# Self attention on one Trainium2 core: score products moved behind the projections on TensorE, their row maxima moved behind the probability split on VectorE

## What is computed

```
q = einsum('btc,hcd->bhtd', x, Wq) + bq;  k, v likewise
scores = einsum('bhtd,bhsd->bhts', q, k) * D ** -0.5
probs  = softmax(scores + causal)          # causal: -inf above the diagonal
y      = einsum('bhts,bhsd->bhtd', probs, v)
x      = x + y @ Wo + bo
```

## Time and profile before

| | us |
|---|---|
| median of 3 runs (1720.44 to 3871.68) | 1721.91 |
| span of the profiled execution | 1720.1 |
| PE busy (TensorE matmul) | 1570.6 (91%) |
| PE weight loads | 1288.7 (75%) |
| DVE busy | 1271.6 (74%) |
| ACT busy | 837.5 (49%) |
| POOL busy | 369.6 (21%) |

### The profile page before, as it was taken

How to read it: one execution, slowest core, us unless ns; L and a number is a source line. 1 busy time by engine, 2 the same in 40 slices (tenths; PEclk the granted TensorE clock), 3 DMA queues, 4 the chain that set the end, 5 groups by cost and what they waited for, 6 DMA issues and landing times. The chain is left out here.

```text
span 1720.1 us, 30317 instructions
## 1 busy us (share of the span) xinstructions
PE 1570.6 (91%) x10720; PEld 1288.7 (75%) x10720; DVE 1271.6 (74%) x2429; ACT 837.5 (49%) x1976; POOL 369.6 (21%) x329
## 2 busy tenths in 40 slices
PE   7886989999999999999999758999999999999996
PEld 5665778778787877878787636877878787878785
DVE  4354687777878778787777857979797979797963
ACT  4443577676776767676676721323232322222220
POOL 2240111021110212111021142313132323232310
PEclk9998999999999999999999978999999999999998
DMA  9998443433434324333432341222212222122000
GB/s 317 330 295 249 89 109 75 99 93 93 116 68 126 74 66 120 89 97 74 110 79 70 111 197 62 74 74 74 73 73 73 73 73 73 73 73 79 19 19 19
DMA packets 75155, 178.52 MB, mean 104 GB/s; under 512 B 9392, under 2 KB 9520, under 8 KB 71344
## 3 DMA queue, kind: packets, MB, share of 16 engines
q1 hardware_dynamic: 75056, 177.07, 34.9%
HBM read 76.37 MB, written 50.33 MB: 74 GB/s over the span
## 5 line engine op out<-in xcount | busy, mean ns | idle before, releaser
L772 DVE TENSOR_REDUCE a_neg_max<-a_score 128x1 f32<-128x384 f32 (+3 forms) x352 | 224.2, 637 | 119.7 <-PE a_score L887 119.0
L676 ACT ACTIVATE a_probs<-a_score,a_neg_max 128x384 f32<-128x384 f32 (+3 forms) x512 | 267.1, 529 | 86.6 <-DVE a_neg_max L772 49.6
L779 DVE TENSOR_TENSOR a_pt_lo<-a_turned,a_pt_hi 128x512 f16<-128x512 f32 (+1 forms) x352 | 223.1, 634 | 12.1 <-ACT a_pt_hi L685 10.6
L896 PE MATMUL a_turned<-ident,a_probs 128*128 128x128 f32 x1280 | 210.7, 283 | 21.6 <-ACT a_probs L676 21.4
L685 ACT ACTIVATE a_pt_hi<-a_turned 128x512 f16<-128x512 f32 (+1 forms) x352 | 197.0, 560 | 64.6 <-PE a_turned L896 64.2
L622 POOL TENSOR_TENSOR a_y<-a_y_sum,a_y_rec 128x128 f32<-128x128 f32 x128 | 51.1, 399 | 661.4 <-DVE a_y_sum L793 661.4
L885 PE MATMUL a_score<-a_stack 96*128 96x384 f32 (+3 forms) x512 | 182.4, 393 | 1.3 <-DMA a_stack<-a_qk 1.3
L916 PE MATMUL a_out_y<-a_v,a_pt_hi 128*128 128x96 bf16 x1280 | 142.5, 209 | 20.8 <-DVE a_pt_lo L779 20.2
L916 PEld LDWEIGHTS a_out_y<-a_v,a_pt_hi 128*128 128x128 f16 x1280 | 98.8, 98 | 81.6 <-issue 44.1
L896 PEld LDWEIGHTS a_turned<-ident,a_probs 128*128 128x128 f32 x1280 | 134.6, 141 | 24.4 <-ACT a_probs L676 24.1
L1133 POOL TENSOR_TENSOR b_probs<-b_probs,b_row_scale 128x1024 f32<-128x1024 f32 x32 | 61.0, 1905 | 361.9 <-DVE b_row_scale L1333 361.9
(11 more groups left out here) (177 smaller groups left out, 4171.3 us busy)
## 6 DMA issues: line engine op xcount, KB each, us to landing
a_stack<-a_qk SPq DMA_DIRECT2D x384, 128.0 KB, 2.4
m_dram<-c_m_out SPq DMA_DIRECT2D x8, 2048.0 KB, 13.2
vw_dram<-shared SPq DMA_DIRECT2D x32, 512.0 KB, 8.4
shared<-m_dram SPq DMA_DIRECT2D x8, 2048.0 KB, 8.1
b_vw_raw<-vw_dram SPq DMA_DIRECT2D x8, 2048.0 KB, 8.4
c_w_raw<-w_group_dram SPq DMA_DIRECT2D x7, 1280.0 KB, 11.2
x_in<-x_dram SPq DMA_DIRECT2D x8, 1024.0 KB, 5.4
a_x_res<-x_dram SPq DMA_DIRECT2D x8, 1024.0 KB, 7.7
```

Source lines behind the costliest of these rows:

```text
L676: ins = nc.scalar.activation(probs[:, n % 2, k * width:(k + 1) * width], score[n % 2][:, k * width:(k + 1) * width], ACT.Exp, bias=neg_max ...
L772: nc.vector.tensor_reduce(neg_max[:, c:c + k], score[n % 2][:, 0:k * width].rearrange("p (h s) -> p h s", h=k), AX, ALU.max, negate=True). ...
L779: nc.vector.tensor_tensor(pt_lo[:, n % 2, 0:width], turned[n % 2][:, 0:width], pt_hi[:, n % 2, 0:width], ALU.subtract).then_inc(pt_ready, 1)
L896: last = nc.tensor.transpose(turned[n % 2][:, c * P:(c + 1) * P], probs[:, n % 2, c * P:(c + 1) * P], ident[:, :])
```

## The change

Three things, all in `self_attention`; nothing is added to or taken from the work.

1. PE: in each unit the steps of the projections are issued ahead of `scores(m + 2)` instead of behind it.
2. PE: inside `scores` all score products of a unit come first, then all causal products. Only the first product of the unit has `start`, only the last has `stop`, since the bank's flags are cleared once.
3. DVE: `row_max(m + 2)` is issued behind `outputs(m - 2)` and `probs_lo(m)` instead of ahead of them.

```diff
@@ DVE, half
                     for kind, n in completed(beside[max(0, m - 1):m]):
                         low_part(it, kind, n)
-                    if unit_at(b, n0 + m + 2):
-                        row_max(*unit_at(b, n0 + m + 2))
                     if unit_at(b, n0 + m - 2):
                         outputs(*unit_at(b, n0 + m - 2))
                     probs_lo(b, n0 + m)
+                    if unit_at(b, n0 + m + 2):
+                        row_max(*unit_at(b, n0 + m + 2))
@@ PE, scores
                 for k, j in enumerate(heads):
                     at = k * width
                     nc.tensor.matmul(score[n % 2][:, at:at + width], st[:, 0, j, i * P:(i + 1) * P], st[:, 1, j, 0:width],
-                                     start=True, stop=False)
+                                     start=k == 0, stop=False)
+                for k, j in enumerate(heads):
+                    at = k * width
                     last = nc.tensor.matmul(score[n % 2][:, at + i * P:at + width], ident_bf[:, :], causal_bf[:, :],
-                                            start=False, stop=True)
+                                            start=False, stop=k == len(heads) - 1)
@@ PE, half
                     turn(b, n0 + m)
+                    for step in beside[m]:
+                        step_of_product(it, *step)
                     if unit_at(b, n0 + m + 2):
                         scores(*unit_at(b, n0 + m + 2))
-                    for step in beside[m]:
-                        step_of_product(it, *step)
                     if unit_at(b, n0 + m - 1):
                         weigh(*unit_at(b, n0 + m - 1))
```

## The result

The changed kernel takes 1825.8 us (median of 4 runs, 1824.66 to 1827.03), against 1721.2 before: ratio 1.0616, 95% interval 1.0601 to 1.0631. Forecast were 1822 us in a range of 1806 to 1846. The ratio leaves out one run of the kernel before that took 3871.68 us; it still counts in the median of 1721.2 us.

A forecast was written before the change was run, and what follows sets the result against it. One round through ACT and DVE per unit was taken to bound the changed kernel: 1720.1 + 96.9 + 1.6 + 2 = 1820.6 us, with 1.8 us up to the median 1822, range 1806 to 1846.

The forecast's parts named there:

- The ring: Self attention: exps, probs_hi, probs_lo, row_max close once per unit on ACT and DVE; 2.55 us per unit, +96.9 us.
- everything beside: Self attention: 1.6 us for DVE's other work in a round plus 2 us for later scores and delayed transposes.
- The term for late scores and full VectorE rounds: Late scores and PE overruns 2 us, bounds 0 and 18; unit 18's crowded DVE round 1.6 us, at most 5.
- The dense stretch: A batch's 21 units with projections: hardly loses, 53 us before and about 53.4 after.
- Where the loss lies: Second half of each batch about 10 us, projection-free half at the end some 22, also first half of batch 0.
- TensorE's term: PE's order: some 28 us less work, bounds 0 and 40, from 18 and 10; counted as 0 in the time.
- the first rival: Self attention: PE stays the bound and its saving comes through, 1720 - 28 = about 1692 us; chance 2%.
- the third rival: Light units: more lost than the round; half clock adds 14 us, with late scores 1840 to 1855 us; chance 12%.
- Signs to look for: Timeline: 2.6 us rounds, exponentials waiting for maxima, PE waiting well over 100 us at transposes; against: clock under 1.00.

The follow-up runs named there:

- the maximum alone: Kernel before with only row_max moved behind outputs and probs_lo on VectorE, TensorE's order old; 1825.9 us, ratio 1.0620.
- the grouping alone: Kernel before with only the causal products of a unit grouped behind its score products on TensorE; 1715.8 us, ratio 0.9958.

## Why the prediction was right

**The ring and its price: right.** The round was summed as 28.03 us per quad. The start-to-start times of the exponentials in the changed kernel add up to 3.35 + 2.87 + 2.73 + 2.38 + 2.14 + 2.14 + 2.28 + 2.38 + 3 x 2.62 = 28.13 us for an undisturbed quad. From the first exponentials (183.1 us) to the last (1086.33) it is 903.2 us against 795.6 before: +107.6 us. The sum had +96.9, and 3.6 for everything beside.

**Some of the closeness is luck.** 107.6 is 7 us more than the 100.5 us counted; outside self attention's steps the changed execution was 4 us shorter (1.8 us ahead of the first exponentials, 2.3 behind the last). No run here gives a cause; the first exponentials start anywhere from 183.1 to 189.1 us in the traces of this case. By the start-to-start times the part beyond +96.9 is 3.2 us since the links of a quad are 0.1 us longer than read, some 3.5 us of overruns (0.5 us a batch in units 1, 20 and 23, where one unit, 18, was named), and 3.7 us in batch 0, whose unit 1 takes 5.24 us and whose units 18 and 19 together take 1.3 us too much: 10.4 us where 3.6 were counted. The term for late scores and full VectorE rounds was too small; its bounds of 5 and 18 us held it.

**The dense stretch: nearly.** From the transposes of unit 0 to those of unit 21 of one batch it took 51.55 us before (590.04 to 641.59) and 53.17 now (638.14 to 691.31): +1.6 us where +0.4 was forecast. Its 53.4 us for the changed kernel was right; its 53 us for the kernel before was the length of the window of the earlier trace rows, not of these 21 rounds.

**Where the loss lies: partly as forecast.** By the starts of the exponentials, the second halves (units 22 to 43) lose 7.6 us each, where about 10 were forecast, the half without projections 21.6 (forecast 22), and the first half of batch 0 11.3. The other seven first halves, said to hardly lose, lose 3.1 us each, 21.5 in all; about half of that is the 1.6 us above. The places' errors cancel, because the round was summed over all 351 steps and not place by place.

**TensorE's term: the sizes at the places were right, the worth was not.** The unit of the earlier trace rows now reads:

```profile
655.36 0.64 PE L901 MATMUL a_turned<-ident,a_probs 128*128 128x128 f32 x4
655.75 0.48 PE L44 MATMUL a_gemm<-a_xt_hi,w_self_hi 128*128 128x512 f32 x1
656.07 0.40 PE L44 MATMUL a_gemm<-a_xt_lo,w_self_hi 128*128 128x512 f32 x1
...
657.25 0.39 PE L888 MATMUL a_score<-a_stack 96*128 96x512 f32 x1
657.48 0.23 PE L892 MATMUL a_score<-a_causal_bf,a_ident_bf 128*128 128x128 bf16 x1
657.55 0.21 PE L921 MATMUL a_out_y<-a_v,a_pt_hi 128*128 128x96 bf16 x1
```

The first projection matmul behind the transposes takes 0.32 us and the score 0.23, where it was 0.32 and 0.31: 0.08 us saved, as written; and the score starts 0.24 us after the last projection matmul, which was a sign to look for. What costs it is the first 512-column fp32r matmul behind 128-column ones (transposes or causal products), of which the unit had two and now has one; whether width or type makes the difference these runs don't tell. In the changed kernel that is worth nothing, since no PE instruction is in the ring: the maximum alone costs as much as the full change. But the first rival's price, "1720 - 28", was wrong: without the ring the two TensorE changes give 1724.9 us. Two things in it failed. The saving was too large even where PE sets the time: both changes take 1.5 us off units 0 to 21 and 0.3 us off units 31 to 44, some 14 us over the eight batches. And not all of a batch is such a place: what was saved ran into the gap at the loop's turn, the transposes ahead of the scores and the lower clock.

**The clock: the third rival's mechanism came, without its price.** The light stretches ran at 0.86 and the last half at 0.68. It was guessed that this could add up to 14 us. The ring, which has no PE instruction in it, hid nearly all of it: in the last half, at a clock of 0.68, all units but one keep the start-to-start times that they have in the middle batches.

**Signs to look for.** Seen: the ring at 2.62 us, maxima that no longer wait for scores (4.8 us, before 119.0), exponentials that wait for the maximum (337 times). Missed: PE's wait at the transposes was forecast "well over 100 us" and is 98.4; the clock inside the stage fell, which was listed as a sign against the forecast, and wasn't one. The last half was forecast at "about 56 us instead of 34" and took 53.6 instead of 32.1 by the exponentials: both 2 us too long, the difference right.

## What to carry to other kernels

Look for rings that go through two in-order engines: follow an instruction to what waits for it and to what stands behind it in its engine's list, until the same instruction of a later unit comes up, and divide the length of the round by the number of units it advances. Swapping two neighbours (here a maximum and a split on VectorE) can take that number from two to one, and then a pair of engines at 46 and 70% busy sets the time, whatever the fullest engine does; start-to-start times from the old trace gave the length of the round to half a per cent (28.03 against 28.13 us) and its cost to a tenth (96.9 against 107.6). Time saved on the fullest engine is worth only what the places behind it don't take back: try the parts of a reordering apart.

## What was not expected of the hardware

- At the turn of the hardware loop TensorE stands still for about 2.5 us (2.50 to 2.68 from start to start in the kernel before, at five turns); ahead of unit 22 of the three other batches, where the loop isn't turned, it is 0.87. With the steps ahead of the scores and no ring it is 3.3 to 3.9 us at the turns and 0.67 else.
- The DMA records tell more of this gap. The trace has a queue "instruction" with packets of 16 KB, and at every turn one of them is under way: in the rows above from 642.61 to 643.79 us before and from 643.21 to 644.18 with both TensorE changes. TensorE's transposes start 1.54 and 1.51 us behind its end, and 1.50 to 1.73 us behind it at all 70 turns of the 14 kernels, though the exponentials that they need had ended at 643.48 and 642.93. The packets elsewhere in the stage come with no such gap (in the kernel before at most 0.95 us). So the gap is most likely TensorE waiting for its own instructions. It grew because the packet starts later: 0.14 us ahead of TensorE's last matmul before, 0.81 us behind it in the other kernel. Why it starts later is not shown.
- At the gaps of 2.4 to 2.8 us the granted clock fell to half at one of five turns before, and at two of five with the grouping alone. At each of the gaps of 2.8 to 3.9 us, in all kernels, it fell to half within 2.3 us of the transposes' start, ahead of it or behind. In the two windows shown around a turn (640 to 660 us with both TensorE changes, 690 to 715 in the full change) it was 0.83 and 0.86, before 1.00. In the earlier trace rows, which begin some units ahead of the half without projections, PE was 33.2 of 39.0 us busy and kept 1.00; at 38.6 of 53.0 us in the changed kernel it got 0.68.
